# Two halves of a batch's P·V product moved into one score burst, with a row of P issued by ScalarE

## The reference, cut to what matters

```
scores = einsum('bhqd,bhkd->bhqk', q, k) / sqrt(32)      # causal
attn   = softmax(scores)
out    = einsum('bhqk,bhkd->bhqd', attn, v)              # the P·V product
```

## Time and profile before

| | us |
|---|---|
| median of 3 runs (lowest, highest) | 1425.23 (1421.73, 1425.78) |
| the profiled execution's own time | 1423.48 |
| its span, first to last instruction | 1421.7 |
| PE busy in the span | 1357.9 (96%) |
| ACT busy in the span | 932.7 (66%) |
| mean granted TensorE clock | 0.985 |

### The profile page before, as it was taken

One profiled execution on the slowest core, in us unless ns is written; L12 is line 12 of the kernel. 1 busy time (PEld: TensorE's weight loads), 2 busy tenths in 40 slices (PEclk: granted clock), 3 DMA queues, 4 the chain that ended last, 5 costly groups with the idle time before them and its releaser, 6 DMA issues. The chain is left out here.

```text
span 1421.7 us, 32292 instructions
## 1 busy us (share of the span) xinstructions
PE 1357.9 (96%) x8288; PEld 1055.6 (74%) x8288; DVE 1096.2 (77%) x3868; ACT 932.7 (66%) x3258; POOL 986.8 (69%) x937
## 2 busy tenths in 40 slices
PE   6899999999999999999975999999999999999985
PEld 4677777777777777777753788888888888888874
DVE  5777878778778777877875688777888777888774
ACT  5778878888788887888874455445555455555442
POOL 3777777777777777777763777667777677776753
PEclk9999999999999999999997999999999999999997
DMA  7335445454453544535466766566666776666651
GB/s 244 108 106 161 131 132 158 115 160 124 137 156 116 162 118 143 152 116 157 131 197 196 193 165 163 158 174 152 160 166 153 166 171 152 162 162 157 155 119 45
DMA packets 108862, 213.04 MB, mean 150 GB/s; under 512 B 26640, under 2 KB 32272, under 8 KB 108816
## 3 DMA queue, kind: packets, MB, share of 16 engines
q1 hardware_dynamic: 108624, 212.25, 54.4%
q10 hardware_dynamic: 192, 0.26, 0.1%
HBM read 131.83 MB, written 34.47 MB: 117 GB/s over the span
## 5 line engine op out<-in xcount | busy, mean ns | idle before, releaser
L452 PE MATMUL wo_ps<-weights,halves 128*128 128x512 f32 x2304 | 572.2, 400 | 11.3 <-DVE weights L630 11.2
L452 PEld LDWEIGHTS wo_ps<-weights,halves 128*128 128x128 f32 x2304 | 422.2, 189 | 148.1 <-issue 59.8
L711 ACT ACTIVATE pexp<-sm,smin 128x128 f32<-128x128 f32 x1024 | 398.4, 393 | 108.8 <-DVE smin L583 104.7
L1067 PE MATMUL wo_ps<-weights,halves 128*128 128x512 f32 x1488 | 399.4, 401 | 4.3 <-DVE yz L1170 4.3
L1420 POOL TENSOR_TENSOR prods<-prod,prods 128x512 fp32r<-128x512 f32 x192 | 260.4, 1364 | 128.0 <-ACT prods L1314 123.1
L840 POOL TENSOR_TENSOR pn<-pexp,prec 128x512 f32<-128x512 f32 x256 | 265.6, 1043 | 99.0 <-DVE prec L590 99.0
L1067 PEld LDWEIGHTS wo_ps<-weights,halves 128*128 128x128 f32 x1488 | 271.9, 189 | 63.2 <-issue 6.0
L583 DVE CUSTOM_DVE_ANT_0 sm<-s_ps,mask_t 128x128 f32<-128x128 f32 x1024 | 231.8, 282 | 24.7 <-PE s_ps L482 23.1
L1314 ACT CAST prods<-prod 128x512 fp32r<-128x512 f32 x192 | 119.0, 622 | 162.2 <-DVE prod L1204 125.6
L1204 DVE TENSOR_TENSOR prod<-att,x 128x512 f32<-128x512 f32 x192 | 188.4, 997 | 10.4 <-DMA att<-sim_scratch 7.6
L711 ACT ACTIVATION_READ_ACCUMULATOR pexp<-sm,smin 128x1 f32 x1024 | 194.3, 190 | 0.0
(11 more groups left out here) (96 smaller groups left out, 1685.3 us busy)
## 6 DMA issues: line engine op xcount, KB each, us to landing
att<-sim_scratch SPq DMA_DIRECT2D x192, 252.0 KB
pt<-blocks SPq DMA_DIRECT2D x636, 64.0 KB, 2.0
ctx_t<-in_ctx SPq DMA_DIRECT2D x32, 576.0 KB, 5.2
raw<-in_xT SPq DMA_DIRECT2D x32, 512.0 KB, 3.9
raw<-ot_scratch SPq DMA_DIRECT2D x32, 512.0 KB, 6.8
xn<-in_x SPq DMA_DIRECT2D x32, 512.0 KB, 7.4
out<-late SPq DMA_DIRECT2D x32, 512.0 KB, 6.3
ot_scratch<-ot SPq DMA_DIRECT2D x63, 256.0 KB, 2.1
```

The source lines that it names most:

```text
L452: mm = pe.matmul(qkv_ps[(par + g) % 2][:], xs[:, par, xl, k], w_sb[:, wl, g, k], start=(k == 0 and n == 0), stop=(k == KT - 1 and n == 2))
L711: ins = nc.scalar.activation(pexp[:, c % 2, i * P:(i + 1) * P], sm[:, c % 2, i * P:(i + 1) * P], ACT.Exp, bias=smin[:, c % 2, i:i + 1], sc ...
L1067: mm = pe.matmul(wo_ps[n][:], os_t[:, par, ol, k], wo_sb[:, wl, k, n * BANK:(n + 1) * BANK], start=(k == 0 and m == 0), stop=(k == KT - 1 ...
```

## The change

The P·V product of a batch gets two PSUM banks: its first half uses `turn_ps`, the bank of the transposes, the second keeps `pv_ps`. Both halves of `b` follow the score burst at slot 13 of the same step, so that nothing of batch `c` is left in a step. The wait for the copy out (`ot_read`) goes from the second half to the transpose of k at slot 17, which writes `turn_ps` next. ScalarE copies both halves out ahead of `exponent(a, 5)`. The four DMAs of the last block row of P's second half go from SyncE to ScalarE in every step, at p 2, ahead of `high_x`, behind a wait for the transposed blocks. SyncE stores the second output half at the end of its step, behind the first half's store, and no longer behind `move_p(b, 1)`.

```diff
-    pv_ps = ps("pv_ps")
+    pv_ps = [turn_ps, ps("pv_ps")]
...
             for qb in range(QB):
-                if at_step(a, B - 1) and u == 1 and qb == QB - 1:
+                if u == 1 and qb == QB - 1:
                     continue
...
             if valid(b):
                 move_p(b, 1)
-            if valid(c) and not at_step(t, LAST):
-                store_later_half(c)
...
                 sp.dma_start(ot_dram[b, :, 0:BANK], ot[:, 0]).then_inc(ot_out[0], 16)
-            if at_step(t, B):
+            if valid(b) and not at_step(t, LAST):
                 store_later_half(b)
...
             wait(pe, p_in[u], after(a, MOVES, MOVES))
             if u == 0:
                 wait(pe, v_in, after(a, 16, 16))
-            wait(pe, ot_read, after(a, NU, u))
+                wait(pe, ot_read, after(a, NU, 0))
...
-                if s == 1 and valid(c) and not at_step(t, LAST):
-                    weigh(c, 1 - par, 1)
                 if s == 1 + NJ * PERIOD and valid(b):
                     weigh(b, par, 0)
-                if s == 17 and (at_step(t, B) or at_step(t, LAST)):
                     weigh(b, par, 1)
                 if valid(t):
                     if s == 17:
+                        if valid(b):
+                            wait(pe, ot_read, after(b, NU, 1))
                         turn_k(t, par)
...
-        def move_last_row():
+        def move_last_row(a):
             qb = QB - 1
-            act.wait_ge(turned, NC * B)
-            act.wait_ge(pv_done, NU * (B - 1))
+            wait(act, turned, after(a, NC, NC))
+            wait(act, pv_done, after(a - 1, NU, NU))
...
             for p in range(NC):
+                if p == 2 and valid(b) and not at_step(t, LAST):
+                    move_last_row(b)
                 if p == 7 and at_step(t, LAST):
-                    move_last_row()
+                    move_last_row(b)
                 if p == 3 and valid(a):
                     copy_q(a, 1)
                 if p == 2 and valid(t + 1):
                     high_x(t + 1, 1 - par)
-                if p == 3 and valid(c) and not at_step(t, LAST):
-                    read_ot(c, 1)
                 if p == 5 and valid(b):
                     read_ot(b, 0)
-                if p == 7 and (at_step(t, B) or at_step(t, LAST)):
+                    if not at_step(t, LAST):
+                        read_ot(b, 1)
+                if p == 7 and at_step(t, LAST):
                     read_ot(b, 1)
```

More of the change, by code:

```diff
@@ L491, in weigh @@
                 wait(pe, v_in, after(a, 16, 16))
-            wait(pe, ot_read, after(a, NU, u))
+                wait(pe, ot_read, after(a, NU, 0))
             for i in range(NI):
                 g = NI * u + i
-                mm = pe.matmul(pv_ps[32 * i:32 * i + 32, :].rearrange("d (j b q) -> d j b q", j=NJ, b=QB),
+                mm = pe.matmul(pv_ps[u][32 * i:32 * i + 32, :].rearrange("d (j b q) -> d j b q", j=NJ, b=QB),
                                v_t[:, par, g * DH:(g + 1) * DH],
@@ L719, in read_ot @@
                 wait(act, ot_out[u], after(a, 16, 0))
-            nc.scalar.copy(ot_last if at_step(a, B - 1) and u == 1 else ot[:, u], pv_ps[:]).then_inc(ot_read, 1)
-        def move_last_row():
+            nc.scalar.copy(ot_last if at_step(a, B - 1) and u == 1 else ot[:, u], pv_ps[u][:]).then_inc(ot_read, 1)
+        def move_last_row(a):
             qb = QB - 1
-            act.wait_ge(turned, NC * B)
-            act.wait_ge(pv_done, NU * (B - 1))
+            wait(act, turned, after(a, NC, NC))
+            wait(act, pv_done, after(a - 1, NU, NU))
             for kb in range(QB):
```

## The result

The changed kernel takes 1475.8 us (median of 6 runs, 1474.49 to 1480.78) against 1425.08 for the kernel before beside it (1420.04 to 1425.78): a ratio of 1.0381, 95% interval 1.0367 to 1.0394, so 3.8% slower. The forecast was 1466 in a range of 1448 to 1487. The profiled execution took 1475.43; its sum of parts is compared with the profiled 1423.48 of before.

A forecast was written before the change was run, and what follows sets the result against it. TensorE bounds, with ScalarE's chain less than 1 us behind; the issues make that chain bind. 28 steps at +1.44 give +40.3, step 2 +1.4, step 31 +1.4, step 32 about -1: 1423.5 + 42 = 1466 us, range 1448 to 1487.

The forecast's parts named there:

- Burst 2: Second score burst of each steady step: forecast at 11.45 us after the first, 0.48 later than now, behind `copy_q(a, 1)`.
- late x: Steady steps: x issued 0.64 us later behind the store, put at 0.1 a step, net +0.05.
- four issues 2.54, and 0.1 for the next instruction: ScalarE ahead of `high_x`: issues done at 8.19 us, `high_x` at 8.3 in place of 6.95.
- The rest of the step: From burst 2 to the next burst 1: the added second half product costs 0.91 us, all else unchanged.
- Step 2: Gets the half product that stood in step 3 and the late `copy_q`: +0.91 + 0.48 = +1.4 us.
- Steps 31 to 33: Last steps: step 31 +1.4 us for issues ahead of `exponent(a, 2)`, step 32 about -1 for a copy leaving the chain.
- No loss: Rival: TensorE stays the bound in every step, 1421 to 1425 us, if `copy_q(a, 1)` ends before 9.9; chance 0.04.
- one switch less a step: TensorE's tiling shape changes once less per steady step: gain 0.08 us a step, 2.2 us over 28.
- Hidden issues, x binds: Rival: ScalarE works on beside its issues and `high_x` starts at x's landing; 1438 to 1458 us, chance 0.13.
- Two queues that wait for one another: Rival: SP's and ScalarE's issues delay each other, four costing 5.1 us; near 1538 us, chance 0.05 fully or in part.
- P late: Rival: P's blocks land up to 1.5 us after the second half product needs them; up to 1500 us, chance 0.04.
- The signs: Right: step near 23.6 us, `high_x` near 8.3 directly behind the issues. Wrong: issues of 1 us and over, step under 22.3.

The follow-up runs named there:

- e9: Kernel before with only the four DMA issues moved to ScalarE ahead of `high_x` in every step; product and stores untouched: 1444.24 us, ratio 1.0153.
- e6: Changed kernel with `copy_q(a, 1)` ahead of `high_x`, first half's copy out one piece earlier, and the store back behind `move_p(b, 1)`: 1431.46 us, ratio 1.0054.
- e10: e6 with the context's load issued behind the moves of P's second half and the store: 1413.8 us, ratio 0.9945 to the kernel before.
- e1: Changed kernel with ScalarE's four issues moved behind `copy_q(a, 1)`: 1461.45 us, ratio 1.0267 to the kernel before.
- e5: Changed kernel with both the four issues behind `copy_q(a, 1)` and the store back behind `move_p(b, 1)`: 1446.82 us, ratio 1.0175 to the kernel before.
- e7: Changed kernel with `copy_q(a, 1)` ahead of `high_x` and first half's copy out one piece earlier; store still ahead of x: 1458.04 us, ratio 1.0242.
- e11: Kernel before with only `copy_q(a, 1)` moved ahead of `high_x` on ScalarE: 1420.26 us, ratio 0.9988.
- e2: Changed kernel with only the second output half's store put back behind `move_p(b, 1)`, so x is sent earlier: 1470.89 us, ratio 1.0345 to the kernel before.
- e8: Changed kernel with three more of SyncE's moves on ScalarE, so seven issues ahead of `high_x`: 1572.73 us, ratio 1.1056 to the kernel before.
- e4: Changed kernel with SyncE issuing all ten moves of P's second half (last batch excepted), store still ahead of x: 1475.4 us, ratio 1.0363.

## Why the prediction was right, and where it was short

The mechanism is the one forecast: four issues ahead of `high_x` take away more than the 1 us that ScalarE had to spare, and what TensorE saves at burst 1 is waited away at burst 2. e9 shows the first half of it alone, e6 and e10 show that burst 2 goes to 9.98 once the copy no longer stands behind the issues and `high_x`. The total was +42 forecast, +51.95 in the profiled executions; three of the four lines of the sum came out larger and the last, by 0.9, smaller, so the forecast's place in its range does not rest on errors that cancelled. Line by line:

- **Burst 2, forecast +0.53 a step with late x, measured +0.71** (11.77 - 11.06). The mis-sized term is "four issues 2.54, and 0.1 for the next instruction": the issues took 2.64 on average (0.66 each, 2.45 to 2.79 in all), and `high_x` followed mostly 0.2 behind them. The start (5.65 forecast, 5.71) and the way from `high_x` to burst 2 (3.15, measured 3.19) were right. Late x, put at 0.1, costs less beside the issues: in the 6 steps where it came last the issues had been done 0.42 on average, 0.22 more than the usual 0.2, so 6 x 0.22 / 28 = 0.05 a step. But it is a second bound close under the first, worth 15 us (e1 against e5) once the issues are out of the way.
- **The rest of the step, forecast +0.91, measured +1.01** (12.28 against 11.27). Where nothing interrupts it, the second half costs 0.86; the remainder is P that landed late in four steps (the product spans 1.67 to 2.43 there), and the sum had P's landing as a rival, as a rule for all steps, with nothing for single ones. In step 21 the idle before burst 2 was 2 us and the clock went down for a while (granted 0.76 from 529 to 536 us), 1.6 more by itself. The sum's 2 us of room before P's last block (11.5 against 13.47) was not there: it took the median of the earlier trace rows for blocks that took 4.6, so the block landed at 13.27, half a us before its use.
- **Step 2, forecast +1.4, measured +3.13** (29.03 against 25.90). Burst 2 is 1.32 later (14.31 against 12.99), and what follows it costs 1.81 more, not 0.91: the term took the full clock's price. PE there, and the window:

```profile
71.53 2.09 PE L480 MATMUL s_ps<-kt,qt 32*128 32x128 f32 x32 [4.24 <-ACT qt L695]
73.55 1.94 PE L493 MATMUL turn_ps<-pt,v_t 128*32 128x512 f32 x8
75.26 1.82 PE L493 MATMUL pv_ps<-pt,v_t 128*32 128x512 f32 x8
```

```profile
70.00:76.00 6.00, 4.46 (x44) 2.39 (x48) 3.56 (x13) 4.19 (x21) 4.72 (x5) 0.50 0.20 51
```

  At a granted 0.50, the lower level, each half takes nearly twice as long, as step 2's half product did before the change too.
- **Steps 31 to 33, forecast +0.4, measured -0.5** with the start of part 2; and step 1 began 1.04 later, ahead of anything that the change touches. That start moves from one execution to the next: it is 35.36 in e9 and 38.95 in e6, which do not differ up to there either.

**The rivals.** *No loss* fell with burst 2 at 11.77; but its condition, `copy_q` done before 9.9, is met in e6, e7 and e10 by the order of two instructions, and e10 then gives more than its 1421. The gain of one switch less a step was put at 0.08; it measured 1.00 removed at burst 1 (2.10 to 1.10) less 0.86 added at burst 2 (2.10 to 2.96), 0.14, and 0.15 between e11 and e10. The drain that the Trainium skill names (TensorEngine Tiling (Array Packing), Key Properties) agrees with that sign. *Hidden issues, x binds* fell as the mechanism of the kernel after, since e2's early x changed nothing in burst 2; e1 is that rival made real, 1461 where it said 1438 to 1458. *Two queues that wait for one another* fell in its full form, and a small part of it is there. ScalarE's issues in the kernel after (ns, shortest, median, longest):

```profile
L725 ACTq DMA_DIRECT2D pt<-blocks x112: 514/619/880, 91.8 to 742.5; - x112
```

Most last what one takes alone, 0.62, and some up to 0.88. In e8 19 of the 97 issues beside SyncE's took over 0.7 us, and 2 of the 99 that had the time to themselves; SyncE's six took 3.84 on average in the kernel after (3.69 to 4.27), where six take 3.73 at the rate of the earlier trace rows. That is some 0.1 us on a row of issues. By the exclusive lock that the Trainium skill describes (Perfetto Trace Analysis, DMA Instruction (HWDGE)) each should last longer beside the other; the trace agrees for a few issues and by little, far from the 0.65 an issue of that rival. *P late* was no rule in the kernel after, but it is what binds next, in e4 to e7.

**The signs.** Those of being right came but one: `high_x`'s idle time is still put down to x's DMA in the waits, also where x had landed up to 1.0 before the CAST and the issues ended 0.2 before it. The steps read one by one and e2, with x early and `high_x` unmoved, decide for the issues. Two of the signs of being wrong showed in single steps: `high_x` right at x's landing in 6, and a gap before the second half product in 4.

## What to carry to other kernels

A DMA issued from a compute engine is work of that engine: count its time per issue, follow what stands behind it in that engine's program order, and put it behind the instruction that the bounding engine waits for. When two events end a wait within half a microsecond of each other, undo both at once before judging either. And when two uses of a buffer are brought together, the data of the later one is needed earlier: see what else is in flight when it is sent.

## What the runs showed of the hardware

A DMA issue holds the issuing engine's later instructions for its whole time, 0.62 us from SyncE and 0.66 on average from ScalarE for a 64 KB block; beside the other queue's issues some last up to 0.88, most don't. Small transfers sent behind a large one are slowed by it: with a 576 KB load issued 1.5 us ahead, 64 KB blocks took 3.6 to 4.2 us to land, and moving that load behind them brought the second half's median from 3.9 to 2.1 and the product's waits from 34.4 us to 2.6. TensorE's clock went to its lower level behind an idle of 4.2 us in step 2, of some 3.6 in every step of e8 (101.3 us in 28), and of 2 us in step 21, though other steps of the kernel after with idles of 1.7 to nearly 2 us kept the granted 1.00. An idle then costs more than its own length: in e8 the rest of the step grew by 1.40 as well.
